# An eight-block transformer chain on one core: the up branch of a quantised feed-forward moves to VectorE and ScalarE, and the first expert mixture is computed with tokens on partitions

## The reference

```python
# block 1: x + _L0_ffn_ref(_layernorm(x), ...)
top_v, top_i = top_k(xf @ router_w.T, 2);  routing_w = softmax(top_v)
for e in range(8):
    w_e = sum(where(top_i == e, routing_w, 0), -1)
    h = gelu(xf @ expert_w1[e].T)                  # (1024, 512)
    out = out + h @ expert_w2[e].T * w_e[:, None]  # (1024, 128)

# block 5: x + _L2_ffn_ref(_layernorm(x), ...)
act_qdq = lambda x: (s := max(max(abs(x)) / 32767, 1e-12), clip(round(x / s), -32768, 32767) * s)[1]
x = act_qdq(x)
up = act_qdq(x @ dequant(w_up).T)                  # (1024, 384)
gate = act_qdq(x @ dequant(w_gate).T)
sig = clip(round(sigmoid(gate) * 65536), 0, 65535) / 65536
gate = act_qdq(gate * sig)
o = act_qdq(gate * up)
return o @ dequant(w_down).T
```

## Time and profile before

| | |
|---|---|
| median of 3 runs | 3732.65 us (3724.59 to 3735.26) |
| profiled execution, its own time | 3727.94 us |
| its span in the trace | 3726.1 us |
| mean granted clock of TensorE | 0.908 of full speed |
| stage 1, from its layer norm to that of stage 2 | 164.5 to 315.4 us |
| stage 5, from its layer norm to that of stage 6 | 2175.9 to 2258.3 us |

### The profile page before, as it was taken

One profiled execution on the slowest core, in us unless ns is written; L12 is line 12 of the kernel. 1 busy time (PEld: TensorE's weight loads), 2 busy tenths in 40 slices (PEclk: granted clock), 3 DMA queues, 4 the chain that ended last, 5 costly groups with the idle time before them and its releaser, 6 DMA issues.

```text
span 3726.1 us, 49832 instructions
## 1 busy us (share of the span) xinstructions
PE 2996.2 (80%) x15209; PEld 990.2 (27%) x15209; DVE 1987.2 (53%) x3503; ACT 1914.4 (51%) x2696; POOL 822.9 (22%) x1339
## 2 busy tenths in 40 slices
PE   6698999986878788787878845878878787888866
PEld 2243333332222222222222211222222222222225
DVE  3313444426557375655837445737465583756624
ACT  4443333334647466564746632746656474665632
POOL 0000444432212222221221221222122122122211
PEclk9898999987989899898989976989999898999987
DMA  1001000001011110100111000111010011101020
GB/s 40 13 32 29 1 1 1 1 12 42 25 30 39 31 38 24 49 25 29 41 31 35 25 13 20 39 31 38 24 49 26 29 40 32 35 26 48 22 111 11
DMA packets 125558, 110.56 MB, mean 30 GB/s; under 512 B 49983, under 2 KB 116077, under 8 KB 125293
## 3 DMA queue, kind: packets, MB, share of 16 engines
q1 hardware_dynamic: 114924, 97.80, 8.9%
q10 hardware_dynamic: 10368, 9.44, 0.8%
HBM read 41.96 MB, written 0.52 MB: 11 GB/s over the span
## 4 chain that ended last, share of the span: by engine, by line
PE 65%; DVE 15%; issue 7%; ACT 6%; POOL 3%; ACTq 2%; SPq 1%; DVEq 0%; DMA 0%; POOLq 0%
PE ps L508 10%; DVE arena L783 7%; PE ps L453 6%; PE ps L482 4%; PE ps L631 3%; PE ps L616 3%; PE ps L574 3%; PE ps L536 3%; PE ps L1435 3%; ACT arena L656 3%; PE ps L560 2%; PE ps L1451 2%; PE ps L525 2%; PE ps L552 2%; PE ps L516 2%
## 5 line engine op out<-in xcount | busy, mean ns | idle before, releaser
L656 ACT ACTIVATE arena<-ps 128x1024 f32<-128x1024 f32 x960 | 936.4, 1024 | 344.7 <-PE ps L482 340.9
L783 DVE TENSOR_REDUCE arena<-ps 128x1 f32<-128x512 f32 x1536 | 967.2, 684 | 206.4 <-PE ps L453 180.4
L508 PE MATMUL ps<-arena 128*32 128x512 f32 x3840 | 512.1, 608 | 20.5 <-ACT arena L656 18.0
L453 PE MATMUL ps<-arena 49*128 49x512 bf16 x1536 | 319.9, 413 | 237.5 <-DVE arena L783 200.6
L482 PE MATMUL ps<-arena 52*128 52x512 bf16 x1920 | 346.1, 386 | 29.0 <-ACT arena L656 25.5
L785 DVE TENSOR_REDUCE arena<-ps 128x3 f32<-128x462 f32 (+1 forms) x576 | 303.3, 580 | 107.4 <-PE ps L460 103.4
L865 POOL TENSOR_TENSOR arena<-arena,zeros 128x16 bf16<-128x16 f32 x192 | 42.2, 220 | 1076.4 <-DVE arena L783 636.6
L453 PEld LDWEIGHTS ps<-arena 49*128 49x128 bf16 x1536 | 75.3, 94 | 588.3 <-DVE arena L783 496.4
L875 POOL TENSOR_TENSOR arena<-arena 128x512 f32<-128x512 f32 x96 | 121.9, 1270 | 451.9 <-ACT arena L688 451.9
L881 POOL TENSOR_TENSOR arena<-arena 128x512 bf16<-128x512 f32 (+1 forms) x84 | 92.4, 1100 | 549.0 <-ACT arena L715 549.0
L803 DVE SCALAR_TENSOR_TENSOR tmp<-tmp,arena,rstd 128x512 f32<-128x512 f32 x72 | 54.1, 752 | 268.8 <-ACT rstd L705 266.5
(11 more groups left out here) (364 smaller groups left out, 4255.3 us busy)
## 6 DMA issues: line engine op xcount, KB each, us to landing
arena<-arena SPq DMA_DIRECT2D x720, 64.0 KB
arena<-we_dram SPq DMA_DIRECT2D x24, 578.5 KB, 8.1
arena<-arena ACTq DMA_DIRECT2D x144, 64.0 KB
w<-weights_dram SPq DMA_DIRECT2D x26, 320.0 KB, 3.0
w<-weights_dram SPq DMA_DIRECT2D x13, 512.0 KB, 3.7
arena<-arena SPq DMA_DIRECT2D x384, 6.0 KB
arena<-arena SPq DMA_DIRECT2D x288, 19.2 KB
w<-weights_dram SPq DMA_DIRECT2D x39, 128.0 KB, 2.2
```

What stands on the lines that cost most here:

```text
L453: pe.matmul(s_bank(slot + r), qst[b][rows, idx, P * qt:P * (qt + 1)], kst[b][rows, idx, :], start=True, stop=True).then_inc(s_full, 1 + (z ...
L508: mm = pe.matmul(bank(7)[32 * j:32 * j + 32, :], v, prob[:, slot, j, :], start=(g % 2 == 0 and kt == 0), stop=(a == 0 and g % 2 == 1 and k ...
L656: act.activation(prob[:, chunk_no(b, a, g, kt) % NPROB, 2 * p:2 * p + 2, :], e_bank(slot).rearrange("p (j n) -> p j n", j=2), ACT.Exp, sca ...
L783: op = ve.tensor_reduce(nmax[:, g % 2, r, n:n + 1], s_bank(slot + r), AX.X, ALU.max, negate=True)
```

## The change

In stage 5 the two GpSimd passes over the up tiles are removed. VectorE makes the first (step up1, rounding left in as value + MAGIC), ScalarE subtracts MAGIC with an Identity activation whose bias is a column of -MAGIC, and up's scale is no longer multiplied into the tiles: the product of the whole numbers of prod and up is taken, and the joint scale (joint5) is applied where the scale of prod was. The all-reduce of up is asked for as before, but its scale and reciprocal are made after the sigmoid steps, behind "all prod"; up1 follows, then prod's scale.

In stage 1 the hidden tiles become the stationary operand of the output product, 128 tokens at a time, and the expert's second weights move. The output then has tokens on partitions, as the gates have, so VectorE multiplies by a column of wsum and adds to acc in one scalar_tensor_tensor of 128x128. The transposes of the gates, the gate rows, their spreading and copies are gone. At the end acc is transposed back by TensorE. All eight experts have their own place in SBUF, the loops are written out, the loads follow each other two at a time, and the outputs of successive experts alternate between banks 4, 5 and 6, 7.

```diff
+        wexp = carve(E1 * MOE_COLS).rearrange("p (r n) -> p r n", r=E1)
+        def moe_hidden_pe(pe, e):
+            pe.wait_ge(expert_loaded[e % 2], 16 * (e // 2 + 1))
+            for f in range(B * FT):
+                b, t = f // FT, f % FT
+                if B * FT * e + f >= 4:
+                    pe.wait_ge(m["hid"], B * FT * e + f - 3)
+                pe.matmul(bank(f % 4), wexp[:, e, P * t:P * (t + 1)], cols(xn, b), start=True, stop=True)\
+                  .then_inc(m["hid_mm"], 1)
+
+        def moe_out_pe(pe, e):
+            for b in range(B):
+                pe.wait_ge(m["hid"], B * FT * e + FT * (b + 1))
+                if e >= 2:
+                    pe.wait_ge(m["added"], 2 * KS * (e - 2) + KS * (b + 1))
+                for n in range(KS):
+                    at = b * S + P * n
+                    for t in range(FT):
+                        mm = pe.matmul(bank(4 + 2 * (e % 2) + b)[:, P * n:P * (n + 1)], hide[:, t, at:at + P],
+                                       wexp[:, e, DFF + P * t:DFF + P * (t + 1)], start=(t == 0), stop=(t == FT - 1))
+                mm.then_inc(m["out_mm"], 1)
+
+        def moe_turn_pe(pe):
+            for b in range(B):
+                pe.wait_ge(m["added"], 2 * KS * (E1 - 1) + KS * (b + 1))
+                for n in range(KS):
+                    tr = pe.transpose(bank(b)[:, P * n:P * (n + 1)], acc[:, KS * b + n, :], ident)
+                tr.then_inc(m["turned"], 1)
...
+        def moe_dve(ve):
+            for e in range(E1):
                 for b in range(B):
+                    ve.wait_ge(m["out_mm"], B * e + b + 1)
+                    for n in range(KS):
+                        i = KS * b + n
+                        out, gate = bank(4 + 2 * (e % 2) + b)[:, P * n:P * (n + 1)], wsum[:, i, e:e + 1]
+                        if e == 0:
+                            ve.tensor_scalar(acc[:, i, :], out, gate, None, ALU.mult).then_inc(m["added"], 1)
+                            continue
+                        ve.wait_ge(m["added"], 2 * KS * (e - 1) + i + 1)
+                        ve.scalar_tensor_tensor(acc[:, i, :], out, gate, acc[:, i, :], ALU.mult, ALU.add)\
+                          .then_inc(m["added"], 1)
+            for b in range(B):
+                ve.wait_ge(m["turned"], b + 1)
+                ve.tensor_tensor(cols(x, b), bank(b), cols(x, b), ALU.add).then_inc(x_ready, 1)
+
+        def moe_sp(sp):
+            for e in range(E1):
+                if e >= 2:
+                    sp.wait_ge(expert_loaded[e % 2], 16 * (e // 2))
+                sp.dma_start(wexp[:, e], dram["we1"][P * e:P * (e + 1), :]).then_inc(expert_loaded[e % 2], 16)
...
         def b1_pe(pe, c):
...
             route_scores_pe(pe, 0)
-            pe.wait_ge(r1["dve"], 9)
-            turn_gates_pe(pe, wsum)
-            moe_pe(pe, c, 1)
+            for e in range(E1):
+                moe_hidden_pe(pe, e)
+                moe_out_pe(pe, e)
+            moe_turn_pe(pe)
         def b1_act(act, c):
...
             act.activation(ratio_e, ratio, ACT.Exp).then_inc(r1["exp"], 1)
...
+            act.preload_act_table_set("gelu_and_others")
+            for e in range(E1):
+                moe_hidden_act(act, e)
...
-            + scales("gate")[1:] + staggered("gate1", "gate2") + [("max_up", i) for i in range(2, TILES5)] + scales("up") \
-            + staggered("sig1", "sig2", "prod", "max_prod") + scales("prod") + staggered("prod1", "out", "max_out") \
-            + scales("out") + [("inv2", "out")] + staggered("out1", "out2")
+            + scales("gate")[1:] + staggered("gate1", "gate2") + [("max_up", i) for i in range(2, TILES5)] \
+            + scales("up")[:1] + staggered("sig1", "sig2", "prod", "max_prod") + scales("prod")[:1] + scales("up")[1:] \
+            + [("up1", i) for i in range(TILES5)] + scales("prod")[1:] + [("whole", "prod")] \
+            + staggered("prod1", "out", "max_out") + scales("out") + [("inv2", "out")] + staggered("out1", "out2")
...
+            then(ve.memset(magic_off, -MAGIC))
...
+            for i in range(TILES5):
+                act.wait_ge(s5["dve"], at5["dve"] + STEP5["up1", i])
+                act.activation(tile5(up5, i), tile5(up5, i), ACT.Identity, bias=magic_off).then_inc(s5["up_whole"], 1)
...
+                elif kind == "whole" and i == "prod":
+                    after(("scale", "prod"))
+                    ve.tensor_tensor(joint5, scale5["prod"], scale5["up"], ALU.mult).then_inc(s5["dve"], 1)
...
+                elif kind == "up1":
+                    after(("inv", "up"))
+                    ve.tensor_scalar(up, up, inv5["up"], MAGIC, ALU.mult, ALU.add).then_inc(s5["dve"], 1)
...
-                    ve.wait_ge(s5["up_scaled"], at5["up_scaled"] + 2 * i + 2)
+                    ve.wait_ge(s5["up_whole"], at5["up_whole"] + i + 1)
...
-            for k in ("x", "gate", "up"):
-                largest(k)
-            gp.wait_ge(s5["dve"], at5["dve"] + STEP5["inv", "up"])
-            for i in range(TILES5):
-                up = tile5(up5, i)
-                gp.tensor_scalar(up, up, inv5["up"], MAGIC, ALU.mult, ALU.add).then_inc(s5["up_scaled"], 1)
-                gp.wait_ge(s5["up_scaled"], at5["up_scaled"] + 2 * i + 1)
-                gp.tensor_scalar(up, up, MAGIC, scale5["up"], ALU.subtract, ALU.mult).then_inc(s5["up_scaled"], 1)
-            for k in ("prod", "out"):
+            for k in KINDS5:
                 largest(k)
```

More of the change, by code:

```diff
@@ L1145, in build @@
         MOE_COLS = 2 * DFF + P + FT + 1
+        E1 = 8
         used[0] = 0
-        wexp = carve(2 * MOE_COLS).rearrange("p (r n) -> p r n", r=2)
+        wexp = carve(E1 * MOE_COLS).rearrange("p (r n) -> p r n", r=E1)
         hide = carve(FT * T).rearrange("p (t n) -> p t n", t=FT)
[L1149 to L1152, removed]
+        acc = carve(T).rearrange("p (t n) -> p t n", n=P)
         moe_end = used[0]
-        m = {k: sem("moe_" + k) for k in
-             ("gate_rows", "hid_mm", "hid", "gate_mm", "gate", "out_mm", "weighted", "added", "start")}
+        m = {k: sem("moe_" + k) for k in ("hid_mm", "hid", "out_mm", "added", "turned")}
@@ L1156, in build @@
         expert_loaded = [sem(f"expert_loaded{i}") for i in range(2)]
[L1157 to L1196, removed]
@@ L1222, in moe_sp @@
[L1222 to L1227, removed]
-                for i in range(2):
-                    sp.wait_ge(m["added"], 4 * q + 2 * (c["experts"] + i + 1))
-                    sp.dma_start(wexp[:, i], dram[name][bass.ds(q * (2 * P) + (2 + i) * P, P), :])\
-                      .then_inc(expert_loaded[i], 16)
+        def moe_hidden_pe(pe, e):
[6 more added lines that the diff above has]
+                  .then_inc(m["hid_mm"], 1)
@@ new lines, in moe_turn_pe, with moe_hidden_act @@
+        def moe_turn_pe(pe):
[4 more added lines that the diff above has]
+                tr.then_inc(m["turned"], 1)
+        def moe_hidden_act(act, e):
+            for f in range(B * FT):
+                b, t = f // FT, f % FT
+                act.wait_ge(m["hid_mm"], B * FT * e + f + 1)
+                act.activation(hide[:, t, b * S:(b + 1) * S], bank(f % 4), ACT.Gelu).then_inc(m["hid"], 1)
@@ L1247, in build @@
         TT = T // P
-        r1 = {k: sem("route_" + k) for k in ("loaded", "mm", "scores", "best", "which", "dve", "exp", "turned")}
+        r1 = {k: sem("route_" + k) for k in ("loaded", "mm", "scores", "best", "which", "dve", "exp")}
         def over_experts(a):
@@ L1837, in build @@
         MAGIC = 12582912.0
+        joint5 = carve(8)[:, 0:1]
         def staggered(*kinds):
@@ L1965, in step @@
                     after(("inv", i))
-                    ve.tensor_tensor(inv5[i], inv5[i], scale5["prod"], ALU.mult).then_inc(s5["dve"], 1)
+                    ve.tensor_tensor(inv5[i], inv5[i], joint5, ALU.mult).then_inc(s5["dve"], 1)
                 elif kind == "x1":
```

51 lines of the change are left out of this document (11 added, 40 removed).

## The result

The changed kernel takes **3684.38 us** (median of 4 runs, 3676.47 to 3700.36) against 3733.95 for the kernel before (4 runs, 3724.59 to 3736.72): 49.6 us less, ratio 0.9877 [0.9837, 0.9917]. The forecast was 27.7 us less and at most some 39. The sign was right. The size was wrong by a factor of 1.8, and the result lies under the range.

The account below looks back on a forecast made before the run. TensorE was taken to bound the first mixture, and VectorE's wait for GpSimd to hold the quantised stage. Terms: -18.0 quantised stage, -9.7 mixture (-8.0 - 17.1 - 1.6 + 1.9 + 15.1), -27.7 from 3732.65: 3705 us, range 3694 to 3718.

Parts of the forecast that it names:

- So 64 x 0.137 = 8.77 us per expert ... 15.1 us more: First mixture, output products: 64 records of 0.137 us per expert against 6.88 us before, 15.1 us more over eight experts.
- record between 0.130 and 0.156: First mixture: spread allowed for the time in us of one 128-column output record, part of the range 3694 to 3718.
- two rows of this very shape agree: Reason for 0.137 us per output record: two short runs of 128x128 f32 products read 0.136 and at most 0.14.
- The gate path, -8.0: First mixture, between router and experts: TensorE goes on at 175.3 and not at 183.30, 8.0 us less.
- Gate spreading and hidden products, -17.1 and -1.6: First mixture: gate spreading goes, 17.1 us less; hidden products take 6.87 us per expert against 7.07, 1.6 us less.
- The low clock, 3.3: First mixture, first hidden products: the lower clock costs 3.3 us again, 1.9 of it new there; lower bound 1.7.
- The end, +-0: First mixture, after the last output product: turning back and adding take as long as before, give or take 0.3 us.
- Stage 5: Quantised stage: without GpSimd's passes and with VectorE's new order, prod1 moves from 2236.91 to 2218.9, 18.0 us less.
- Narrow products that eat the mixture's gain: First mixture, rival: at 0.156 us per output record the mixture gives nothing, total 3714.7 us; chance 0.10.
- a load that isn't hidden (0.216): First mixture, rival: output records cost load plus stream, 0.216 us each, total 12.7 us slower at 3745; chance 0.03.
- The reload before the prod all-reduce: Quantised stage, rival: GpSimd's 6.60 us idle returns before that all-reduce, losing 4.2 of 18.0 us, total 3709.2; chance 0.03.
- narrow records at their stream rate or an early clock: First mixture, rival: output records run at stream rate or the clock rises early, up to 15 us more gain, 3690; chance 0.04.

Follow-up runs that it names:

- The two runs with small products: The changed kernel with an extra product of 8 moving columns ahead of each four output products: 3714.8 us with weights of 8 rows, 3695.65 with 128.

## Why the prediction was right or wrong

**The step that failed: "So 64 x 0.137 = 8.77 us per expert ... 15.1 us more".** The record takes 0.1116 us. 512 x (0.137 - 0.1116) = 13.0 us, of the 14.0 by which stage 1 beat its sum. With 0.1116 in it the forecast would have been 3692, already under the range's 3694. The range's "record between 0.130 and 0.156" left the true value out, though the text had named 0.107 as the lower bound.

Why the rows read 0.137: both runs in the earlier trace rows are short, and each took in something besides records of this shape. The run of 8 was timed to the start of the next line, whose weights have another shape (49 rows). The run of 12 was divided with the whole length of its last record in it, and it isn't one run: the timeline merges a line's records, and the view that keeps shapes apart (window 357.9 to 359.5) shows ten of 128x128 and two of 26 weight columns:

```profile
L1390 PE MATMUL ps<-arena 128*128 128x128 f32 x10 | 1.4, 285 | 0.0
L1390 PE MATMUL ps<-arena 128*26 128x128 f32 x2 | 0.4, 282 | 0.0
```

The weight loads of the run of 8 tell the record from the step behind it:

```profile
2337.48 0.97 PEld L585 LDWEIGHTS ps<-w,xn 128*128 128x128 f32 x8 [0.23 <-issue]
2338.57 0.10 PEld L453 LDWEIGHTS ps<-arena 49*128 49x128 bf16 x2
```

The load of the last record is in the 0.97 us, but not the step to the next shape. With one load of 0.19 us at the end (what a single 128x128 f32 load lasts in the trace), the spacing is (0.97 - 0.19)/7 = 0.111. The ten loads of the other run start 0.111 us apart too. So the price was in the trace of before: 8 x 0.1116 = 0.89 us of records and some 0.2 of turning to the next shape make the 1.09 us to the next line. The same 0.2 stands ahead of the two records of 26 columns, where the number of rows stays at 128: the last load of the ten and the next one start 0.31 us apart, not 0.11. A change of columns does it as well as one of rows. The two runs with small products show the turning by experiment, for rows. The prediction argued that "two rows of this very shape agree"; they agreed by accident, one with the turning spread over 8 records, the other with a turning and the length of the last record over 12.

The 64-column records of the earlier trace rows had more to say than a bound on the load. Eight of them in a row, in another place of the same stage, have this row of weight loads:

```profile
3691.14 0.97 PEld L2093 LDWEIGHTS ps<-h,arena 128*128 128x128 f32 x8
```

It is as long as that of the 128-column records above. The added products of 8 columns with weights of 128 rows cost 0.19 us for two records over the stage, and 1.12 - 8 x 0.1116 = 0.23 between one and the next. So a f32 record with its own 128x128 load costs 0.10 to 0.11 us at 8, 64 and 128 columns alike. The load, or something else that each record pays once, sets that price and not the columns; these show at 512, with 0.430.

The Trainium skill (TensorE: Matmul & The Clock Gate, "Wait — 56ns, not 53.3ns?") gives 55.6 ns from start to start at 128 columns and 215.7 at 512, both at full clock. In that proportion the measured 0.430 of 512 columns makes 0.111 at 128, as an estimate, and the chain's 0.1116 agrees with it, though by the 64-column row the columns are not what sets it. The Trainium skill (TensorE: Matmul & The Clock Gate, "Back-to-back issue gap") gives 81 and 131 ns where every product has its own load, a proportion that these records (0.26 between the two widths, not 0.62) do not show.

That turning is also what the prediction noted without a cause: the 0.2 us by which hidden products were dearer "where products of 8 rows alternate with those of 128". In the earlier trace rows it shows at both ends, 1.91 - 4 x 0.43 = 0.19 us in the spreading and 7.07 - 6.87 = 0.20 in the hidden products, somewhat more than in the runs with small products.

The rest of stage 1:
- *The gate path, -8.0.* Right. From the last addition before it to the first product of the experts' loop: 183.30 - 164.4 = 18.9 us before, 179.31 - 168.5 = 10.8 after, 8.1 less.
- *Gate spreading and hidden products, -17.1 and -1.6.* Right. The spreading is gone and the hidden products take 6.87 us.
- *The low clock, 3.3.* It cost 9.20 - 6.87 = 2.3 us: the records after 188.51 run at full speed (granted clock 0.79 over 179 to 190, 1.00 from there). 1.0 us better.
- *The end, +-0.* From the end of the last output product to the start of the last addition: 295.7 - 293.8 = 1.9 us, before 315.3 - 313.3 = 2.0. 0.1 better.
- Sum: 9.7 + 13.0 + 1.0 + 0.1 + 0.1 = 23.9, for 23.7 measured.

**Stage 5** was right in each step: the new order of VectorE, up1 (2.47 us for six, 2.4 forecast), the all-reduce hidden behind it, ScalarE's six subtractions covered, and no table load before the first. The stage gave 1.4 more than the sum. 0.3 of it is in prod1; 1.1 is in the last products, 12 records that took 8.08 us in the kernel before and 7.00 in the changed one. There the clock rises earlier in the group. The windows of the 2 us that begin 2.5 us into it, first of the kernel before (columns as in the earlier trace rows):

```profile
2252.00:2254.00 2.00, 2.00 (x4) 0.78 (x3) 0.91 (x3) 0.00 (x0) 0.00 (x0) 0.50 0.00 0
```

then of the changed kernel:

```profile
2227.50:2229.50 2.00, 2.00 (x5) 0.91 (x4) 0.97 (x4) 0.00 (x0) 0.00 (x0) 0.81 0.00 0
```

The granted clock is 0.50 in the one and 0.81 in the other. Nothing in the prediction forecast this 1.1 us; the change didn't aim at it, and that it helped is luck. Passing between tensor_scalar and the all-reduce costs 5.90 to 7.05 us where it shows at all.

**The rivals.** Narrow products that eat the gain (0.156) and a load that isn't hidden (0.216) are both ruled out by 0.1116. The load's price, bounded in the prediction at 0.109, is about what the record costs: load and stream lie side by side. By the rule that the prediction took from the Trainium skill (TensorE: Matmul & The Clock Gate, "The mechanism"), loads would not overlap here; the chain's 7.14 us for 64 speaks against that more clearly than the rows of before did. The reload before the prod all-reduce did not come back; the kernel with a tensor_scalar in front of it shows what it would have cost, 4.0 us on prod1 (4.2 in the prediction). The rival that came nearest had a chance of 0.04: "narrow records at their stream rate or an early clock", up to 15 us more. The two together gave 14.0 in stage 1.

**The other stages.** By the profiles the two stages explain 42.9 to 44.8 us of 49.6 (first comparison), 51.7 and 43.9 (the changed kernel on two more chips). On the last chip 1 us is left over. The changed kernel's three medians lie within 1.5 us (3684.4, 3682.9, 3683.1); those of the kernel before beside it are 3734.0, 3734.6 and 3727.1. So what goes beyond the two stages comes and goes with the kernel before. No profile of it was taken on the chip with 51.7, so which of its stages was longer there stays open, and the part of a median above 44 us isn't explained by the change.

The profiles, for their part, show no gain outside the two stages but a loss. The six other stages together took 3490.3, 3488.9 and 3487.9 us in three profiles of the kernel before and 3505.8, 3497.1 and 3495.0 in three of the changed one, each of these the slowest run of its four. Most of it is stage 4, and there it isn't even scatter: all seven profiles with the new mixture and no added products have 1353.0 to 1363.7 us, the six others 1345.7 to 1348.8. Stage 4 has no edit in any of them. Its time at the lower clock is 238.9 to 273.1 us in the seven and 221.9 to 238.9 in the six, so the clock goes with it without explaining all. What makes the difference is not shown; the two kernels with small products, which have the new mixture too, are among the six.

## What to carry to other kernels

A price per instruction read from a short run of them should end with that run's own last start, or with its weight loads, not at the start of what follows: a change of shape there is a cost of its own, and dividing it by eight makes it look like a rate. A timeline row that merges records can hold two shapes, so ask for the shapes apart before dividing. Products of few rows among products of all rows cost the turning twice, so group them or give them away. And where a bound (here 0.107) and a reading (0.137) are far apart in a term taken 512 times, the range must hold both.

## What the runs showed that was not expected

**GpSimd's memsets hold a small VectorE cast.** In stage 3 eight memsets run back to back on GpSimd while VectorE casts 128x8 whole numbers. The changed kernel:

```profile
757.63 16.09 POOL L1773 MEMSET arena<- 128x4096 bf16 x6 [7.90 <-DVE x L1604]
...
769.27 6.68 DVE L1740 CAST arena<-arena 128x8 f32<-128x8 uint32 x1
...
773.65 2.28 POOL L1775 MEMSET arena<- 128x1280 bf16 x2
```

The cast takes 6.68 us and ends at 775.95, with the last memset (775.93). In each of the eleven profiles in which nothing holds the memsets back it ends within 0.04 us of the end of one of them. In the three profiles of the kernel before it took 0.90, 0.81 and 1.11 us, in the changed kernel 6.68, 6.76 and 2.25. With the fourth and later memsets held back (second chip):

```profile
757.27 10.42 POOL L1775 MEMSET arena<- 128x4096 bf16 x3 [8.33 <-DVE x L1604]
...
771.00 0.17 DVE L1740 CAST arena<-arena 128x8 f32<-128x8 uint32 x1
...
771.23 5.73 POOL L1775 MEMSET arena<- 128x4096 bf16 x3 [3.54 <-DVE arena L1740]
```

it takes 0.17 us, as on the other chip. Other steps of VectorE beside the memsets, eight MAX8 (0.64 us together) and tensor_tensors (0.22 us each), take the same in both kernels. Stage 3 went from 42.2 to 49.2 us in the first profile of the changed kernel, though the change doesn't touch it. What decides how long the cast is held stays open: in the three profiles of the changed kernel it began equally far into the memsets, 11.6 us after the first one's start, and was held 6.68, 6.76 and 2.25 us. The Trainium skill (GPSIMD Engine Reference, "1. Specifications") says that GpSimd's SBUF interfaces are shared with VectorE, and that VectorE's steps in a 2-port performance mode or with two SBUF inputs contend. The rows agree that something is shared, with 6.68 us against 0.17. The cast has one input, so the second case is not its own; whether it runs in such a mode, no run here shows.
